# Four short stretches between the layers of a graph network put in another order

## The reference, cut to what matters

```python
x = _layernorm(x + attention(x, src, dst, edge_weight, edge_attr))        # layer 0: segment softmax over edges
x = _layernorm(x + relu((concat[x, mean of x[src] over dst] @ W1 + b1) @ W2 + b2))     # layer 1
x = _layernorm(x + segment_sum((x @ weight[rel])[src], dst))              # layer 2: 8 relations
# layer 3
agg = concat[relu(x), for t in 3: segment_sum(where(edge_type == t, relu(x[src] @ W_e[t].T + b_e[t]), 0), dst)]
x = _layernorm(2 * x + (agg @ W_n[node_type].T + b_n[node_type]))
```

## Time and profile before

| | |
|---|---|
| median of three runs | 1652.73 us (1651.75 to 1653.54) |
| profiled execution | 1652.15 us |
| its span | 1650.4 us |
| busy: PE, DVE, ACT, POOL | 1388.8, 1419.0, 1110.9, 1230.3 us |
| mean granted TensorE clock | 0.929 of full speed |

### The profile page before, as it was taken

One profiled execution on the slowest core, in us unless ns is written; L12 is line 12 of the kernel. 1 busy time (PEld: TensorE's weight loads), 2 busy tenths in 40 slices (PEclk: granted clock), 3 DMA queues, 4 the chain that ended last, 5 costly groups with the idle time before them and its releaser, 6 DMA issues.

```text
span 1650.4 us, 22899 instructions
## 1 busy us (share of the span) xinstructions
PE 1388.8 (84%) x6078; PEld 890.6 (54%) x6078; DVE 1419.0 (86%) x3056; ACT 1110.9 (67%) x2769; POOL 1230.3 (75%) x910
## 2 busy tenths in 40 slices
PE   3788877788778868777776899999996899999995
PEld 2455554555545546666665555555553455555552
DVE  5899899999899879999998799999995677777773
ACT  1678788887788787888888577777774344444441
POOL 7888888877777857888874567777778488888873
PEclk9798888988889879999998999999998899999997
DMA  7344444434444256767675455556554344344320
GB/s 172 94 100 102 111 109 110 112 91 115 111 113 105 58 139 177 189 179 192 182 187 149 131 149 164 156 157 165 151 133 111 83 97 96 96 97 97 96 70 20
DMA packets 165797, 205.06 MB, mean 124 GB/s; under 512 B 66825, under 2 KB 97920, under 8 KB 165668
## 3 DMA queue, kind: packets, MB, share of 16 engines
q1 hardware_dynamic: 108068, 179.45, 40.0%
q0 software_dynamic: 57600, 24.15, 9.0%
HBM read 147.12 MB, written 70.80 MB: 132 GB/s over the span
## 4 chain that ended last, share of the span: by engine, by line
PE 44%; DVE 32%; ACT 12%; issue 10%; POOL 1%; DMA 1%; SPq 0%; DVEq 0%; POOLq 0%; ACTq 0%
PE po L1391 23%; DVE bst L756 8%; DVE masked L969 6%; PE pt L1380 5%; PE pc L1500 3%; PE po L1386 3%; ACT x L1074 3%; DVE run L831 2%; PE po L1451 2%; DVE y L796 2%; DVE po L799 2%; DVE sel L802 2%; DVE po L800 2%; ACT do L1074 2%; PE pa L1672 1%
## 5 line engine op out<-in xcount | busy, mean ns | idle before, releaser
L536 POOL DMA_INDIRECT xs<-target_rows,slot_all x236 | 322.2, 1365 | 140.9 <-issue 60.9
L1074 ACT ACTIVATE x<-y,nmr,rst 125x128 f32<-125x128 f32 x800 | 322.5, 483 | 29.6 <-issue 18.4
L1391 PE MATMUL po<-wnt,rt 128*125 128x384 f32 x800 | 297.4, 518 | 0.0
L1380 PE MATMUL pt<-ident,x 125*128 125x125 f32 x800 | 122.3, 276 | 110.5 <-issue 110.5
L1391 PEld LDWEIGHTS po<-wnt,rt 128*125 128x125 f32 x800 | 162.7, 206 | 96.9 <-issue 21.2
L1391 PE MATMUL po<-wnt,run 128*125 128x384 f32 x600 | 201.5, 486 | 0.0
L543 POOL DMA_INDIRECT out_rows<-do,last_all x100 | 146.5, 1465 | 63.0 <-issue 40.6
L1380 PEld LDWEIGHTS pt<-ident,x 125*128 125x128 f32 x800 | 93.1, 145 | 148.4 <-issue 147.1
L536 POOL DMA_INDIRECT xs<-in_x,src_all x100 | 143.2, 1432 | 34.7 <-issue 33.8
L1074 ACT ACTIVATE do<-yd,nmr,rst 125x128 f32<-125x128 f32 x400 | 163.5, 483 | 5.4 <-DVE nmr L781 4.6
L1074 ACT ACTIVATE res<-sel,nmr,rst 125x128 f32<-125x128 f32 x400 | 163.7, 484 | 2.6 <-DVE nmr L781 1.8
(11 more groups left out here) (190 smaller groups left out, 3035.1 us busy)
## 6 DMA issues: line engine op xcount, KB each, us to landing
xin<-in_x SPq DMA_DIRECT2D x100, 224.0 KB
out_rows<-res SPq DMA_DIRECT2D x100, 224.0 KB
source_rows<-so SPq DMA_DIRECT2D x75, 224.0 KB
target_rows<-do SPq DMA_DIRECT2D x75, 224.0 KB
xs<-source_rows SPq DMA_DIRECT2D x59, 224.0 KB
same<-same_d SPq DMA_DIRECT2D x50, 250.0 KB
rel<-in_etype SPq DMA_DIRECT2D x50, 250.0 KB
xd<-target_rows SPq DMA_DIRECT2D x46, 224.0 KB
```

The costliest lines, as they stand in the source:

```text
L536: return nc.gpsimd.indirect_dma_start(out=to, out_offset=None, in_=table, in_offset=bass.IndirectOffsetOnAxis(ap=index, axis=0), bounds_ch ...
L1074: last = A(to[:, j, :], y[:, j, :], ACT.Identity, scale=rst[s][:, k:k + 1], bias=nmr[s][:, k:k + 1])
L1380: last = nc.tensor.transpose(tile_of(to, j), rows_[:, j, :], ident[0:R, 0:R])
L1391: last = mm(po[0:R, j * 512:j * 512 + NT * D], left(j), wnt[:, k, :, :].rearrange("k t d -> k (t d)"), start=start, stop=stop, skip_group_ ...
```

## The change

No instruction is added or taken away; 4 places get another order, on three engines.

- ACT, border of layers 0 and 1: the bank of x3's turn is emptied before the last source rows are scaled, that of x1's turn behind them; `first_roots` of dense step 50 goes ahead of two tiles of results. `dense_chain` is split for this in two, with `chain_rows` as its second part.
- PE, border of layers 1 and 2: the turn of chunk 0's sources (`turns2(0)`) goes ahead of `dense_products` of step 75.
- ACT, border of layers 2 and 3: `st` of chunk 1 is taken out before the last dense chain, not behind it.
- POOL: beside the last five chunks of layer 1, where no `slot_all` is left to fetch, three types each are fetched. 15 of the 17 types that stood between layers 2 and 3 are thereby gone from there.

```diff
@@ POOL, layer 1's loop
                     slots1(i, i + 1, s_slot[k])
+                if SOONER * T + 3 * c >= EC * T:
+                    types2(typed, typed + 3)
+                    typed += 3
             types2(typed, typed + 2 * T)
@@ ACT
             def dense_chain(d):
 
+                first_roots(chain_of(d) % 2, 4)
+                chain_rows(d)
+
+            def chain_rows(d):
+
                 k = chain_of(d)
-                first_roots(k % 2, 4)
                 act.wait_ge(s_ln, k + 1)
                 rows_of(d, k % 2, (2, 0))
                 results_of(d, k % 2, 1)
@@ ACT, last chunk of layer 0
                     target_rows0(c, TAIL, 0)
+                    evacuate_rt(2 * EC - 2)
                     source_rows0(c, s)
+                    evacuate_xt(2 * EC - 2)
+                    first_roots(chain_of(2 * EC) % 2, 4)
                     results_of(2 * c, s, 2)
                     results_of(2 * c + 1, s, 3)
...
-            only_dense(2 * EC)
+            chain_rows(2 * EC)
@@ ACT, ahead of layer 3
             targets3(0)
+            evacuate_sources(1, 3, 0)
             dense_chain(NC + 2 * LAG - 1)
-            evacuate_sources(1, 3, 0)
@@ PE, ahead of layer 2
             dense_turns(d - 2)
-            dense_products(d - 2)
             pe.wait_ge(ph[1]["rd"], EC)
             turns2(0)
+            dense_products(d - 2)
             relations2(0, range(REL // 2))
```

## The result

| | before | changed |
|---|---|---|
| median | 1652.95 us (1651.75 to 1653.54, 4 runs) | 1638.40 us (1637.34 to 1639.48, 4 runs) |
| profiled execution, its span | 1652.15, 1650.4 us | 1638.99, 1637.2 us |

The ratio is 0.9913, with an interval of 0.9897 to 0.9929: 14.5 us less, where 19.4 were forecast (1633.3 us, range 1629.5 to 1643). The changed kernel run again beside the experiments took 1638.03 us against 1653.68 (ratio 0.9901, 0.9885 to 0.9917), 15.6 less.

A forecast was written before the change was run, and what follows sets the result against it. PE bounds layer 3 and DVE's chain the layers before, so only the borders can gain: 0.7 + 4.7 + 14 = 19.4 us off 1652.15, predicted 1633.3 us with the median's 0.58 offset, range 1629.5 to 1643 (own mechanism 1630 to 1635.5).

The forecast's parts named there:

- Border 2 to 3: Layers 2 to 3: moved types, earlier `st`; PE's second chunk 15.1 us sooner; 14 taken, bounds 8.3 and 15.5.
- both steps: Last border: DVE's three scans 7.2 us sooner; 8.3 gained if PE still starts cold and only the order of `st` helps.
- Rival 1: Clock stays at half through the border of layers 2 and 3: gain there 10.5, sum 15.9, time 1637; chance 0.16.
- Rival 2: Gathers land too late at borders 1 to 2 and 2 to 3: gains 2 and 8.3, time 1641.7; chance 0.15.
- Rivals 3 and 4: 3: POOL becomes layer 3's bound, 1668, chance 0.04; 4: load or store chain sets layer 3's pace, 1652, chance 0.03.
- Border 1 to 2: Layers 1 to 2: PE's source turns ahead of dense products start layer 2 sooner; 4.7 us gain, bounds 2 and 5.3.
- Chunk 0's last gather ends ... at 909.7, lands at 911.3: Border 1 to 2: gathered rows land about 1.6 us behind POOL's end, so PE's source turns run at 911.3, not 916.62.
- The dense products behind end at 917.1 ... hidden: Border 1 to 2: products moved behind the source turns end before DVE, their first reader, needs them at 919.8.
- Border 0 to 1: Layers 0 to 1: ACT empties the bank sooner, so PE turns sooner; 0.7 us gain, bounds 0 and 1.4.
- the z that DVE's next read needs, with some of the products at half clock, 0.7 us sooner: Border 0 to 1: z comes 0.7 us sooner despite half clock after PE's new 4.4 us idle; the term's basis.

## Why the prediction was right in sign and too high by 5 us

**Border 2 to 3: right.** The mechanism, both steps (7.2 and 8.3 forecast, 7.43 and 8.64 measured) and the sum of 15.1 hold; 14 had been taken for late gathers, and they were not late. Rival 1 (half clock through) fell: without a pause ahead of it the turn took 0.62 us, and the clock stood at 1.00 through the border. (Its time has 0.6 us twice: 1652.15 less 15.9 plus 0.58 is the 1636.8 already.) Rival 2 came true at the other border alone. Rivals 3 and 4 fell with the unchanged window of layer 3: POOL kept pace in the new phase. (The stretched scatter of 1.95 us in the earlier trace rows, which rival 3 puts beside DVE's masks, stands beside its scans, from 1444.14 to 1447.70.)

**Border 1 to 2: the mechanism held, its size did not; 4.7 was 1.6, outside its own lower bound of 2.** One term was mis-sized, and one that came out right had nothing to spare.
- "Chunk 0's last gather ends ... at 909.7, lands at 911.3": the landing was 5.58 us, not 1.64, a figure carried over from a border with less traffic (a DMA share of 0.34 from the last gather to PE's turn, against 0.96 here). Counted from scan 99, the last gather ended at 21.4 (forecast 909.7, that is 22.4) and the turn stood at 26.96 (forecast 24.0): 2.9 us late. That is nearly the 3 us of the stated lower bound; 4.7 less 2.9 is 1.8, and it had been put at 2.
- "The dense products behind end at 917.1 ... hidden": hidden from DVE's read, but not from PE, whose next source turn stands behind them. The forecast had that turn at 925.0, 13.7 us behind the first, and 13.74 were measured, so this cost nothing against the forecast. But it is luck of the clock: turn to scan 100 was 16.63 us before, is 17.35 and 17.07 in the changed kernel, and was up to 18.59 in kernels with the same order there, where the products ran colder; these show a loss at this border. With the turn 2.40 us sooner after scan 99 and 0.72 more from the turn to scan 100, 1.68 of the difference is accounted for.

**Border 0 to 1: the forecast gain of 0.7 was a loss of 0.6 to 0.9, outside its own lower bound of 0.** Every time up to the next turn came within 0.6 us of the forecast, and the first scan even 1.3 us sooner (from scan 72: 47.27 against 48.58; forecast 1.0). The step that failed is "the z that DVE's next read needs, with some of the products at half clock, 0.7 us sooner". The second pause does not make some of them slow but nearly all (turns 1.07 us, biases 1.48, types 4.60; only z's own products ran warm, 1.04), and DVE waits 2.1 us for z, more than the whole gain. The pause filled, z is in time.

**Sum.** -0.7, -4.7, -14 became +0.7, -1.7, -15.1: 16 us by the two traces, where 19.4 were forecast: 1.6 and 3.1 too much at the first two borders and 1.3 too little at the last, by the first trace. By the medians it was 14.5 and 15.6 (by the intervals 11.7 to 17.0 and 13.7 to 19.0), since the part ahead of the first edit varies by 5 us between executions. The time, 1638.4, lies in the stated range but outside the 1630 to 1635.5 that the forecast kept for its own mechanism. It is nearest to rival 1's 1637, and rival 1 did not occur: that is chance: the late gathers of rival 2 at one border alone and a loss at the first border happen to add up to it.

## What to carry to other kernels

- When work is moved on an engine, ask of that engine itself, not only of the readers, whether it had the idle time to take it, and at which clock it will run.
- Cutting one long pause of PE in two can cost more than it saves, since here each piece was followed by slow work; look at what stands behind the second.
- A small gather that the next stage waits for should land before bulk loads and stores are issued, even if these are then some us late: here one wait on the issuing queue was worth 2.9 us at its border, and the two reorderings that touch it 1.6 together. Check a few chunks on that the held loads are not asked for.

## What the runs showed of the chip

- The rows of four small indirect gathers are there 1.53 us behind POOL's end at a DMA share of 0.07 and 1.64 us at 0.34, but 5.0 to 6.3 us behind it at 0.81 to 0.96.
- The same stretch of PE has a cold part whose length changes. In the two executions of the changed kernel the type products behind the first of the two pauses took 3.19 and 4.40 us, those behind chunk 0's turn at the border of layers 1 and 2 3.32 and 3.06; in kernels with the same code at that place the latter took up to 4.60, where full clock is 2.74. This alone moves that border by 1.5 us. One profile of each kernel is not enough to compare them to a us.
- Idle products of constants keep the clock up as real ones do: the turns ahead of them were warm (0.59 and 0.62 us), the clock stayed at 1.00 over 7.15 and 4.02 us of them, and the turn behind took 0.59 us, against 1.07 behind a pause of 4.92 or 4.34. Whether they would raise a clock that has fallen, no run shows.
